# A decoder block on one core: another order in cross-attention, and products that no one reads

## The reference

```python
x = x + _L0_attn_ref(_layernorm(x), ...)              # self-attention, 16 heads of 32
x = x + _L0_xattn_ref(_layernorm(x), ctx_1024, ...)   # cross-attention
x = x + _L0_ffn_ref(_layernorm(x), ...)               # 8 experts, top 2
# inside the second:
rel = jnp.abs(jnp.arange(Nk)[None, :] - jnp.arange(Nq)[:, None] - (Nk - Nq))
scores = jnp.einsum('bhqd,bhkd->bhqk', q, k) * scale - slopes[:, None, None] * rel
out = jnp.einsum('bhqk,bhkd->bhqd', softmax(scores), v) @ Wo + bo
# inside the third:
w_BSN = softmax(x @ Wr.T + br); _, idx = top_k(..., 2)  # weights of the two, divided by their sum
y = sum over the two experts of weight * (silu(a) * b) @ Wl2 + bl2,  [a, b] = x @ Wl1 + bl1
```

## Time and profile before

| what | value |
|---|---|
| median of the runs shown | 1781.89 us (1773.87, 1781.89, 1784.19) |
| the profiled execution, its own time | 1781.67 us |
| its span | 1780.0 us |
| mean granted clock of PE | 0.973 of full |
| opening, middle, cross, experts start at | 0, 163, 679, 1164 us |
| busy PE, DVE, ACT, POOL | 1685.4, 1075.7, 748.0, 751.6 us |

### The profile page before, as it was taken

How to read it: one execution, slowest core, us unless ns; L and a number is a source line. 1 busy time by engine, 2 the same in 40 slices (tenths; PEclk the granted TensorE clock), 3 DMA queues, 4 the chain that set the end, 5 groups by cost and what they waited for, 6 DMA issues and landing times. The chain is left out here.

```text
span 1780.0 us, 34824 instructions
## 1 busy us (share of the span) xinstructions
PE 1685.4 (95%) x11064; PEld 1356.9 (76%) x11064; DVE 1075.7 (60%) x1895; ACT 748.0 (42%) x1345; POOL 751.6 (42%) x852
## 2 busy tenths in 40 slices
PE   7998999999999997998998998789999999999998
PEld 6887787887887776776776776578888888888876
DVE  5453565555556654877878887663664646445653
ACT  3224343344344425665655564522442424224441
POOL 3100323323333325977788656541542414115451
PEclk9999999999999997999999998989999999999999
DMA  7836766666576758997877766245673737346773
GB/s 216 254 134 170 205 185 179 184 177 173 165 196 176 197 148 162 188 221 157 172 152 164 154 150 157 85 126 169 187 245 101 242 102 241 105 133 212 235 251 89
DMA packets 211841, 309.52 MB, mean 174 GB/s; under 512 B 21856, under 2 KB 151600, under 8 KB 207232
## 3 DMA queue, kind: packets, MB, share of 16 engines
q1 hardware_dynamic: 191584, 232.40, 49.3%
q0 software_dynamic: 15392, 41.02, 10.4%
q10 hardware_dynamic: 4752, 34.61, 5.3%
HBM read 224.30 MB, written 83.66 MB: 173 GB/s over the span
## 5 line engine op out<-in xcount | busy, mean ns | idle before, releaser
L2155 DVE TENSOR_REDUCE part_max<-a_s_bank 112x1 f32<-112x500 f32 (+1 forms) x368 | 225.3, 671 | 61.5 <-PE a_s_bank L1884 41.8
L2050 ACT ACTIVATE a_prob<-a_st_bank 125x448 f32<-125x448 f32 x384 | 196.7, 546 | 117.8 <-PE a_st_bank L1905 93.8
L2855 DVE TENSOR_TENSOR e_u_sb<-e_u_bank,e_b_row 128x512 f32<-128x512 f32 x134 | 92.4, 689 | 231.7 <-PE e_u_bank L2612 216.4
L2610 PE MATMUL e_u_bank<-e_w_hi,e_xT_hi 128*128 128x512 f32 x536 | 215.3, 402 | 0.9 <-DVE e_w_lo L2848 0.4
L2611 PE MATMUL e_u_bank<-e_w_lo,e_xT_hi 128*128 128x512 f32 x536 | 210.9, 393 | 0.0
L2612 PE MATMUL e_u_bank<-e_w_hi,e_xT_lo 128*128 128x512 f32 x536 | 210.4, 392 | 0.0
L2671 ACT ACTIVATE e_g_hi<-e_g_bank 128x256 fp32r<-128x256 f32 x133 | 51.3, 386 | 342.0 <-PE e_g_bank L2619 334.5
L2772 POOL DMA_INDIRECT out<-l_rows,e_y_row x33 | 53.0, 1605 | 290.7 <-DVE l_rows L2898 162.8
L1752 POOL TENSOR_TENSOR a_part_sum<-a_prob 125x448 f32<-125x448 f32 x128 | 148.2, 1162 | 54.5 <-ACT a_prob L2050 53.4
L992 POOL TENSOR_TENSOR m_prob_sum<-m_prob 112x224 f32<-112x224 f32 x128 | 85.4, 671 | 161.8 <-ACT m_prob L1240 152.1
L2748 POOL TENSOR_TENSOR e_w_lo<-e_w_raw,e_w_hi 128x1024 fp32r<-128x1024 f32 x28 | 102.6, 3674 | 49.0 <-ACT e_w_hi L2681 49.0
(11 more groups left out here) (413 smaller groups left out, 4368.7 us busy)
## 6 DMA issues: line engine op xcount, KB each, us to landing
e_w_raw<-L_ffn_Wl SPq DMA_DIRECT2D x96, 512.0 KB, 11.0
e_b_row<-L_ffn_bl ACTq DMA_DIRECT2D x33, 1024.0 KB
k<-m_kt_hi SPq DMA_DIRECT2D x48, 250.0 KB, 4.1
k<-m_kt_lo SPq DMA_DIRECT2D x48, 250.0 KB, 5.0
m_c_in<-ctx POOLq DMA_DIRECT2D x12, 896.0 KB, 6.7
v<-m_cv SPq DMA_DIRECT2D x48, 224.0 KB
a_v_sb<-v SPq DMA_DIRECT2D x32, 336.0 KB
m_q_st<-q SPq DMA_DIRECT2D x93, 112.0 KB, 3.1
```

The costliest lines, as they stand in the source:

```text
L2050: act.activation(prob[s % 2][:, hh, 2 * u:2 * u + 2, :], st_bank[n % SB][0:CR, 0:2 * S].rearrange("p (e q) -> p e q", e=2), ACT.Exp).then_ ...
L2155: dve.tensor_reduce(out, scores, AX.X, ALU.max).then_inc(s_free, 1)
L2610: pe.matmul(out, xT_hi[:, slot, k, :], w_h, start=(k == 0), stop=False)
L2855: dve.tensor_tensor(u_sb[:, q % 2, :, :], u_bank[q % 2][:, :].rearrange("p (h n) -> p h n", h=2), b1_row[:, slot, :, HC * q:HC * q + HC], ...
```

## The change

1. Products that no one reads are added on PE, into banks that are free: 8 at the end of the opening, 10 at the end of the middle; in cross-attention 4 in front of the first `first_scores`, 3 ahead of each of the `second_scores` of steps 0 and 1, 6 and 3 in `turn_max(0)` and `(1)`, 4 in `turn_max(31)`, 10 and 8 in the last step.
2. In the middle ACT does `minus_max(s)` ahead of `keys_hi` in its first two steps.
3. SP issues Wo after the queries, keys and values of steps 4 and 5, and the biases and the zeros of the place table later. The first `add_out_bias` is moved from s = 3 to s = 4.
4. At s%4 = 0, from s = 4 on, POOL splits between the sums of heads 0, 1 and of heads 2, 3. Its stores of entries are dealt out anew: 6, 6, 4 at s = 27, 28, 29.
5. The first go moves from s = 20 to 22, and `choose`, `slots` and `weights` of batches 0 to 3 are spread over other steps. The second go stays.
6. In the last step POOL neither sums nor splits: PE sums over six probability tiles (24 products in place of 16), DVE does the last two splits, and both do their rest in another order; the fourth `split_w1` moves into `moe_phase`.

The core of the diff:

```diff
@@ middle, ACT
+                        if s < 2 and hh == 0:
+                            minus_max(s)
                         if unit_at(s, hh) is not None:
                             keys_hi(unit_at(s, hh))
-                        if hh == 0:
+                        if s > 1 and hh == 0:
                             minus_max(s)
...
-    GOES = {20: (0, 8), 28: (8, FIRST_TILES)}
-    RANKED = {20: 3, 28: 2}
+    GOES = {22: (0, 8), 28: (8, FIRST_TILES)}
+    RANKED = {22: 3, 28: 2}
+    STORED = {27: (0, 6), 28: (6, 12), 29: (12, 16)}
@@ SP
-                load_qk(SLOTS)
-                load_v(SLOTS - 1)
+                for s in (SLOTS, SLOTS + 1):
+                    load_qk(s)
+                    load_v(s - 1)
                 sp.dma_start(w_raw[:, :, :], w_out.rearrange("(k p) n -> p k n", p=P)).then_inc(w_loaded, DMA)
@@ POOL
-                    if s + 1 < STEPS:
-                        sums(s + 1)
-                    if s:
+                    if s >= 4 and s % 4 == 0:
+                        sums(s + 1, range(0, 2))
                         split_o(s - 1)
+                        sums(s + 1, range(2, 4))
+                        if s in STORED:
+                            store_entries(0, *STORED[s])
+                    else:
+                        if s + 1 < STEPS - 1:
+                            sums(s + 1)
...
-                    if s == 3:
+                    if s == 4:
                         pool.wait_ge(bias_loaded, DMA)
                         add_out_bias(0)
@@ PE
+                def keep_clock(bank, n):
+                    for _ in range(n):
+                        pe.matmul(bank[:, :], w_hi[:, 0, 0:P], w_hi[:, 0, :], start=True, stop=True)
...
-                    if t == 0:
-                        pe.wait_ge(osplit_ready, GROUPS * b + g1)
+                    pe.wait_ge(osplit_ready, GROUPS * b + g1)
...
+                keep_clock(or_bank[0], 10)
+                turn_h(B - 1)
+                route(B - 1)
+                keep_clock(or_bank[0], 8)
@@ DVE
-                        if s == 13:
-                            if hh == 0:
-                                choose(0, 2, 0)
-                                choose(0, 2, 1)
...
+                        if (s, hh) in ((13, 0), (13, 2), (14, 1), (14, 3), (15, 1)):
+                            choose(0, 2, 2 * (s - 13) + hh // 2)
+                        if s == 21:
+                            choose(2, 4, hh)
+                        if (s, hh) == (22, 0):
+                            choose(2, 4, 4)
+                        if (s, hh) == (22, 3):
+                            slots(22, 0)
...
@@ DVE, behind the loop
                 split_w1(0)
-
-                dve.wait_ge(pv_done, STEPS - 1)
-                split_w1(1)
                 normalise(STEPS - 2)
-                normalise(STEPS - 1)
+                split_o(STEPS - 2)
...
+                split_w1(1)
+                normalise(STEPS - 1)
+                split_o(STEPS - 1)
...
-                for q in range(2, HCH):
-                    split_w1(q)
+                split_w1(2)
...
```

More of the change, by code:

```diff
@@ L466, in _ @@
                             first_scores(hh)
+                n = len(prod_at)
+                pe.wait_ge(o_free, n - OB + 1)
+                for _ in range(8):
+                    pe.matmul(o_bank[n % OB][:, :], w_hi["wv"][:, 0, 0:P], w_hi["wv"][:, 0, :], start=True, stop=True)
             @block.scalar
@@ L1222, in _ @@
                     cross_scores(n)
+                pe.wait_ge(cross_done, 14)
+                for _ in range(10):
+                    pe.matmul(cross_bank[16 % 3][:, :], w_hi["wq"][:, 0, 0:P], w_hi["wq"][:, 0, :], start=True, stop=True)
             @block.scalar
@@ L1743, in add_out_bias, with sums @@
                                        ALU.add).then_inc(xb_ready, 1)
-                def sums(s):
+                def sums(s, heads=range(4)):
                     w = s % 2
-                    if s >= 2:
+                    if s >= 2 and 0 in heads:
                         pool.wait_ge(pv_done, s - 1)
-                    for hh in range(4):
+                    for hh in heads:
                         pool.wait_ge(st_free, st_at["s", s, hh, 1] + 1)
@@ L1863, in st_next, with keep_clock_early @@
                     return st_bank[n % SB]
+                def keep_clock(bank, n):
+                    for _ in range(n):
+                        pe.matmul(bank[:, :], w_hi[:, 0, 0:P], w_hi[:, 0, :], start=True, stop=True)
+                def keep_clock_early(bank, n, s):
+                    for _ in range(n):
+                        pe.matmul(bank[:, 0:LIN], k_st[s][0:KD, 0, 0:P], k_st[s][0:KD, 0, 0:LIN], start=True, stop=True)
                 def first_scores(s, hh, n):
@@ L1984, in turn_wr @@
                 def turn_wr():
[L1985 removed]
+                    pe.wait_ge(wr_loaded, DMA)
                     bank = st_next("wr")
@@ L2371, in _ @@
                 split_w1(0)
-                dve.wait_ge(pv_done, STEPS - 1)
-                split_w1(1)
                 normalise(STEPS - 2)
-                normalise(STEPS - 1)
-                scores_done(B - 2)
-                for part in range(5):
-                    choose(B - 2, B - 1, part)
-                for t in range(2):
-                    residual(B - 1, t)
-                moments(B - 1)
-                hidden(B - 1)
+                split_o(STEPS - 2)
                 dve.wait_ge(table_loaded, DMA)
@@ L2389, in _ @@
                     dve.tensor_copy(x_row[:, st:st + 1], table_sb[:, st, 0:1]).then_inc(x_row_ready, 1)
-                for q in range(2, HCH):
-                    split_w1(q)
+                split_w1(1)
+                normalise(STEPS - 1)
+                split_o(STEPS - 1)
+                scores_done(B - 2)
+                for part in range(5):
+                    choose(B - 2, B - 1, part)
+                for t in range(2):
+                    residual(B - 1, t)
+                    moments(B - 1, (t,))
+                hidden(B - 1)
+                dve.wait_ge(xhi_ready, 1)
+                dve.tensor_tensor(xT_lo[:, 0, :, :], or_bank[1][:, :].rearrange("p (k n) -> p k n", k=KT), as_f32(xT_hi[:, 0, :, :]), ALU.subtract).then_inc(t_free, 1)
+                split_w1(2)
                 scores_done(B - 1)
```

135 lines of the change are left out of this document (73 added, 62 removed).

## The result

The changed kernel is slower. Its median is 1792.77 us (1783.64 to 1798.41, 11 runs), that of the kernel before, measured beside it, 1778.67 us; the ratio is 1.0071, with a 95% interval of 1.005 to 1.0092, so 9 to 16 us more. In a second session it was 1.0065 (1.004 to 1.0089). The forecast was 12.7 us less, with a range that ended at 1785.

What follows compares the result with a forecast made beforehand. PE was taken as the bound, busy for 1685 of 1780 us. The terms -1.5 + 1.5 - 4.4 + 0 - 4.5 - 2 - 1.8 = -12.7 took 1781.67 to 1769.0 us, range 1754 to 1785.

Steps and rivals of the forecast that it cites:

- E: Steps 13 to 15: choose(0,2) spread over three steps instead of all in step 13; 0 us, +-1.5.
- F: Steps 19 to 26: dealing out choose(2,4), slots and weights saves a third of their 13.4 us; -4.5 us.
- B: Cross-attention's start: Wo too late +1.5, earlier queries and keys -2.6, late output bias +2.6; sum +1.5 us.
- The third part: Cross-attention's start: the later output bias makes the first residual late and PE needs its bank; +2.6 us.
- D: Step 9's projection: the earlier POOL split at s%4 = 0 removes PE's wait and half clock; -4.4 us.
- The third rival: Cross-attention's start: Wo comes late, ACT stands 6.2 us, the kernel is slower, +5.2 us, 1786.9 us; chance 0.07.
- A: The middle's start and opening's end: PE's wait for ACT goes, little of the clock gain counted; -1.5 us.
- G: Steps 27 to 29: with the stores moved, L2247 runs free of POOL's adds; -2 us.
- H: The last step: one split of weights instead of two behind the norm, no POOL sums or splits; -1.8 us.
- three signs of being wrong: Steps 19 to 26 as long as before, experts' phase changed by over 3 us, Wo waited for over 4 us.

Runs made afterwards that it cites:

- e3: The kernel before with only choose(0,2) spread over steps 13 to 15; 1.0055 of the kernel before.
- a4: The changed kernel with all five parts of choose(0,2) back in step 13; 1.0033 of the kernel before.
- b4: The kernel before with only the change's order of loads and the late first add of the output bias; 1.001 of the kernel before.
- a3: The changed kernel with Wo issued early again and the output bias added in step 3 again; 1.0015 of the kernel before.
- a6: The changed kernel with the loads' order, the first bias add and all choices of experts as before; 0.9969, then 0.9955 of the kernel before.
- d1: a6 without all products that no one reads; 0.9959, then 0.9997 of the kernel before.
- d2: a6 with POOL's split behind all eight adds again at s%4 = 0; 0.9995 of the kernel before.
- d3: a6 with the last step as before the change; 0.9979 of the kernel before.

## Why the prediction was wrong

**E, choose(0,2), failed first.** I had "the same instructions on the engine that is late there, in three steps for one", and 0 +-1.5. It costs 5.1 us between the two traces, 0.55% (10 us, 7 to 13) by itself in e3, and undoing it gave back 0.3 to 0.4% in a4. The step that failed is the pricing of a moved instruction by its duration at the old place. In step 13 the counts stand where POOL has ended its adds, 0.76 us; in step 15 they stand beside them, 2.60 us, DVE's maxima are late, PE waits 2.29 us for them, and its clock is 0.69 in the 5 us from 909 us. The rule that would have told it was in my own text: the Trainium skill (GPSIMD Engine Reference, Key points) says that POOL contends with DVE instructions that have two SBUF inputs. The trace agrees, 0.76 against 2.60 and 2.62 us for the same four instructions. I had laid it on one instruction, L2247, and not on all that the change moves past POOL's adds. And the trace of before shows it for the counts too, those of `choose(2,4)` in step 20, with PE's wait behind them:

```profile
970.88 2.93 DVE L2232 TENSOR_TENSOR r_before<-r_before,r_mask 112x8 f32<-112x8 f32 x4
```

```profile
974.69 0.76 PE L1884 MATMUL a_s_bank<-third 100*112 100x500 f32 x1 [2.79 <-DVE part_max L2155]
```

These two rows showed E's mechanism before the change was run. The stretch at a clock of 0.51 on which F rests begins here, at 973 us.

**B, cross-attention's start,** forecast +1.5. From the first load to the end of step 5 the two traces of the change have +8.5 and +7.4 us. As a forecast of Wo's wait it was too small, 7.27 us against 1.5: counted from the first load, Wo landed at 57.8 us where the forecast has 54.4, and ACT stood ready for it at 50.6 in place of 52.7. Yet that wait is not the main cost: b4, with a wait of 3.37 us for Wo, is at 1.001, and undoing Wo's place gave 0.25% at most. The stretch from the first load to step 4 hardly follows the order of the loads: 78.2 us before, 81.1 and 80.3 with the change, 80.3 in a3 and 75.4 and 78.5 in a6 with the order undone. The third part, the late bias, had the right chain (split, four adds, the bias, the residual), but its size was 5.6 us and not 2.6: the residual was late by less, 0.5 us against before, but the whole step stood earlier, and PE's 2.61 us of wait was followed by 7 us at a clock of 0.51, which I had left out of the sum. And it shows only together with D: 17.8 us in step 5 in b4, 21.8 to 23.3 in the five traces with both.

**The third rival** named this place and the ACT wait (6.2 us, measured 7.27), and its sign came true. Its reason did so in part: Wo lands late, but with Wo early `second` does, and the loss that stays is the late bias's and E's, which it had at 4.2 us and at nothing.

**A** was -1.5; -1.2 and +0.5 were read, within the scatter of the same code, so it is neither shown nor refuted: the wait for ACT went, and a wait for a load of 2.86 us took its place. **The added products** hold the clock as meant (0.87 in place of 0.50 in the last step; the eight transposes at 1162.62 take 0.98 us in place of 1.76), and a6 against d1 shows no time from it. I had feared the transposes there, since the Trainium skill (TensorE: Matmul & The Clock Gate, Part 4) says that they don't count as work for the clock as matmuls do. Here the clock stood through them in ten of the twelve traces with products ahead of them (0.98 or 0.99 us for the eight; 1.34 and 1.45 in d2 and the second of a6), and they took 1.22 to 1.76 us in the eight without.

**D** was right in its mechanism: steps 6 to 12 fell by 3.3 and 4.2 us, and d2 gives 0.4%; that batch 0 has no such wait holds for the trace of before, not for d2's. **F** was -4.5; it is -0.6, and 117.4 us lies within the 116.9 to 118.7 of the traces with the old choices. As E, the parts stand beside adds wherever they are put: in the changed kernel the counts of batches 2 and 3 took 3.68 us, PE stood 4.53 us for the maxima in step 22, and at a clock of 0.51 from 1003 to 1010 us. **G**: L2247 came free of the adds, 0.15 us in every trace with the new stores and 2.50 to 3.01 in the four with the old ones, and steps 27 to 29 took 0.8 us more, not 2 less. Both traces have an unnamed wait there, that of before one of 4.05 us on ACT; in those without it the three steps take 51.6 to 53.9 us with the new stores and 51.3 to 53.0 with the old, so G gives nothing that shows. The wait in step 28 is in seven of the sixteen traces with the new stores and in none of the four with the old; whether they bring it isn't tested. **H** was -1.8; the last step is worth 0.24%, 4 us, by d3.

So the terms on which the gain rested were worth: A and its products nothing that is shown, D -3 to -7, F and G 0, H about -4. Against them stand E, +5 to +10, and the bias behind the early split, +5 to +9. By the ratios, the loads and the bias undone take the change from 1.0071 and 1.0065 to 1.0015 (a3), the choices undone too to 0.9955 and 0.9969 (a6): some 9 us each, against some 7 that the rest gives. Two of the forecast's three signs of being wrong came, the wait of over 4 us for Wo and steps 19 to 26 as long as before; the third, the experts' phase, didn't.

The fastest version that was measured twice with the same outcome is a6, the change without its order of loads, its late bias and its choices: 0.9955 and 0.9969 of the kernel before in two sessions, about 7 us less.

## What to carry to other kernels

Before a small vector instruction is moved, look at what the neighbouring engine does at the new place: here four additions with two operands in SBUF took 1.8 us longer beside POOL's adds, and their place was worth 0.4% of the kernel. Where the DMA share is above 1 over a stretch and an engine waits for whichever load is last, price the stretch from its first load as a whole; here another order of the loads was worth 0 to 0.25%, and a faster clock of the engine that waits nothing that showed. And price moved parts together: alone the late bias cost nothing and the early split gave, and together they cost 5 us in one step. Before a stretch of a single trace is explained, look at how far it varies with the same code: step 3 took 15.4 to 20.9 us in five such traces.

## What was not expected of the hardware

Four additions on 112x8 took 0.76 us where POOL had no add and 2.04 to 3.68 us beside its adds, while POOL's own of 125x448 kept their 1.13 to 1.16 us. The time of the opening, with the same instructions but for its last eight products, varied from 159.3 to 164.2 us between profiles. In the profile of before the clock is 0.91 from 50 to 70 us and 0.89 from 110 to 125, where the changed kernel's has 1.00. And in 7 of the 20 traces PE halts in a row of sixteen column sums in step 28 without waiting for anything that the trace names, and ACT stands 4.93 to 6.48 us behind it.
